# Layer 3's query norm by a block transpose and one folding product per head, and its scores scaled on ScalarE

## The chip, the cores and the metric

The kernel runs on one core of one Trainium2 chip. The metric is the time of one execution in microseconds, taken on the device; the number given is the median of several runs.

## The reference, cut to what matters

The program is four decoder layers over 1024 tokens of width 512 (8 tiles of 128 tokens). Each layer adds a gated cross attention and then a gated feed-forward to x:

```python
x = x + tanh(g_xattn[l]) * attention_l(layernorm(x), ctx)
x = x + tanh(g_ffn[l]) * ffn_l(layernorm(x))
```

The change lies in the attention of the third layer (index 2; "L2" in the code), which has 32 query heads of 128 features, 8 key heads, and per batch of 128 queries 128 keys:

```python
q = rmsnorm(hidden @ q_proj_w.T per head, q_norm_w)   # x * rsqrt(mean(x*x over 128 features) + 1e-5) * w
k = rmsnorm(ctx @ k_proj_w.T per head, k_norm_w)
scores = einsum('bhqd,bhkd->bhqk', q, k) / sqrt(128) + attention_mask
out = einsum('bhqk,bhkd->bhqd', softmax(scores), v) @ o_proj_w.T
```

The norm of a query row is one number per token and head. The kernel leaves the queries unscaled and multiplies the scores of that token by it instead; both norm weights are folded into the keys.

## The kernel before, in words

All engines run their own instruction streams, written out in Python in one order for each engine, and meet in semaphores. There is no planner: the order of the work is the order of the code. A projection splits its operands into a high and a low part (`w_hi`, `w_lo`, `xt_hi`, `xt_lo`, `a_hi`, `a_lo`) and takes three products per 128 rows of depth (`mm3`). GpSimd makes the two parts of each weight chunk (L558, L562) from a ring of 8 chunks, as soon as TensorE has freed a slot (`w_free`); SP loads the raw chunks.

An attention runs in 64 steps (`run_steps`, here with a period of 8 steps), two for each of the 32 heads: step k holds 4 of the 8 batches of head k // 2. In step k each engine does, in this order:

- TensorE (`step` in `attention`): the scores of step k into a bank of S, the turn of the probabilities of step k - 1 (`turn`, L930), the outputs of step k - 2 for two token tiles, three quarters of one half (512 tokens) of the next head's query projection into a bank of J, the outputs for the other two tiles, the last quarter of the projection, the product of the probabilities of step k - 1 with the values (`values`), and `q_squares`: for the half just projected, four products of a 128x128 block of squares (stationary) with a column of ones, which give the sum of squares per token.
- ScalarE: the copy of the turned probabilities of step k - 1 (`turned_out`), the exponentials of step k (four, each with its sum), then for the projected half the squares into `sq` (L1317) and the copy to `qT`, then `a_hi` of step k - 1 from the bank of the values.
- VectorE: four fused operations (L1816), each one batch's scores times the query norm plus the mask, the row maxima (L1824), the adds of the outputs to x for tiles 0 and 1 (L1767), the reciprocal of the sums and its product with the gate (L1846, L1849), the adds for tiles 2 and 3, and `a_lo` of step k - 1 (L1866). Between these stand, one at a time, the 12 small instructions of `query_rstd`: an integer first guess and three Newton steps (L1532 to L1540) that turn the sums of squares of one half into the norm `rq`. They are dealt out by `small(a, b)`.

The outputs of step k - 2 need `a_hi` and `a_lo` of that step: `output` waits for both. The bank of the values may be rewritten when both are made. An output for a tile waits until the tile two before it, in the same bank, has been added to x.

In the prologue of the layer (`L.first`) come values and keys, the layer norm of x, and the two halves of head 0's query.

A matmul on 4-byte data runs as two passes in the trace, so that four products with the ones are eight rows.

## Time and profile before

| | |
|---|---|
| time, three runs | 2902.35 to 2905.36 us, median 2904.11 us |
| the profiled execution: its span | 2904.7 us |
| the profiled execution: its time beside the span | not listed apart from the span |
| instructions | 47006 |
| TensorE busy | 2778.9 us, 96% |
| VectorE busy | 1728.2 us, 59% |
| ScalarE busy | 1048.6 us, 36% |
| GpSimd busy | 826.4 us, 28% |

In the profile PE is TensorE's matmul queue and PEld its weight loads, DVE is VectorE, ACT is ScalarE, POOL is GpSimd. Times are microseconds unless marked ns. Matmuls are pipelined, so that the start of one to the start of the next says what one costs. PEclk is the granted clock of TensorE as a share of full speed. A number in brackets on a timeline is the time for which the engine was idle before the instruction, with what ended the wait.

### The profile page before, as it was taken

Reading aid. Unit: us, or ns where it says so; the run is one execution under the profiler, and the core shown is the slowest. Engines: PE = TensorE matmul, PEld = TensorE weight load, DVE = VectorE, ACT = ScalarE, POOL = GpSimd, SP = SyncE. Lnnn points to the kernel's source line nnn. Section 1 sums busy time; section 2 is a strip of 40 time slices with the busy share of each in tenths; the row PEclk is TensorE's granted clock in tenths of the full one; section 3 lists DMA queues with packets and bytes.
Section 4 is the critical chain, followed back from the end, with each engine's and each line's share of the span. In section 5 each row is a group of like instructions: output and inputs, shape, how many; then the busy total and the mean of one; then the engine's idle time right before and its main releaser. Section 6 shows DMA issues by size and latency. Waiting matters only on the chain.

```text
span 2904.7 us, 47006 instructions
## 1 busy us (share of the span) xinstructions
PE 2778.9 (96%) x14928; PEld 2337.4 (80%) x14928; DVE 1728.2 (59%) x3969; ACT 1048.6 (36%) x2828; POOL 826.4 (28%) x708
## 2 busy tenths in 40 slices
PE   7997999999999998889999999999999999999998
PEld 5875888888888886667888888778878888888886
DVE  5756545544644646667777777745552555555557
ACT  3542333333333332124444444321123444444442
POOL 4011432432442431322222222245522222212200
PEclk8998999999999999999999999999999999999999
DMA  4001111111110110111111111012111000001000
GB/s 145 12 12 53 41 44 33 47 36 32 47 41 28 51 44 19 45 30 33 30 30 30 31 31 30 26 41 58 58 45 40 27 27 26 27 26 27 29 5 30
DMA packets 59826, 106.35 MB, mean 37 GB/s; under 512 B 7184, under 2 KB 11536, under 8 KB 59536
## 3 DMA queue, kind: packets, MB, share of 16 engines
q1 hardware_dynamic: 56448, 96.49, 11.6%
q10 hardware_dynamic: 3216, 7.81, 0.8%
q8 instruction: 87, 1.43, 0.2%
q14 instruction: 75, 0.61, 0.1%
HBM read 100.09 MB, written 2.10 MB: 35 GB/s over the span
## 4 chain that ended last, share of the span: by engine, by line
PE 90%; DVE 6%; ACT 2%; issue 2%; DMA 0%; POOL 0%; ACTq 0%; DVEq 0%; POOLq 0%
PE four L587 51%; PE outp L587 23%; PE value L587 9%; PE turned L930 4%; PE turned L709 1%; DVE stats L1565 1%; DVE xt_lo L1594 1%; PE turned L634 0%; DVE nt L1537 0%; DVE nt L1539 0%; DVE probs L1589 0%; DVE x L1767 0%; DVE x L1973 0%; ACT sq L1317 0%; ACT vc L1203 0%
## 5 line engine op out<-in xcount | busy, mean ns | idle before, releaser
L558 POOL TENSOR_TENSOR w_hi<-raw,zero 128x512 fp32r<-128x512 f32 x347 | 371.8, 1072 | 1926.3 <-PE four L587 896.4
L1767 DVE SCALAR_TENSOR_TENSOR x<-outp,g_inv,x 128x512 f32<-128x512 f32 x768 | 556.6, 748 | 383.5 <-PE outp L587 383.2
L562 POOL TENSOR_TENSOR w_lo<-raw,w_hi 128x512 fp32r<-128x512 f32 x352 | 454.0, 1290 | 32.3 <-ACT w_hi L1203 5.1
L587 PE MATMUL four<-xt_hi,w_lo 128*128 128x512 f32 x1024 | 424.8, 415 | 16.8 <-DVE xt_lo L1594 12.0
L587 PE MATMUL four<-xt_hi,w_hi 128*128 128x512 f32 x1024 | 406.2, 397 | 0.0
L587 PE MATMUL four<-xt_lo,w_hi 128*128 128x512 f32 x1024 | 404.4, 395 | 0.0
L587 PE MATMUL outp<-w_hi,a_lo 128*128 128x512 f32 x800 | 330.3, 413 | 14.3 <-DVE x L1767 7.5
L1203 ACT ACTIVATE pT<-turned 128x512 f32<-128x512 f32 x320 | 191.6, 599 | 345.1 <-PE turned L930 287.3
L587 PE MATMUL outp<-w_hi,a_hi 128*128 128x512 f32 x800 | 316.0, 395 | 0.0
L587 PE MATMUL outp<-w_lo,a_hi 128*128 128x512 f32 x800 | 315.3, 394 | 0.0
L1396 ACT ACTIVATE probs<-probs,top 128x128 f32<-128x128 f32 x512 | 199.6, 391 | 237.6 <-DVE top L1810 126.7
L587 PE MATMUL four<-kT,qT 128*128 (+2 forms) x1536 | 275.8, 316 | 6.5 <-issue 6.5
L1866 DVE TENSOR_TENSOR a_lo<-value,a_hi 128x512 fp32r<-128x512 f32 (+1 forms) x256 | 142.9, 558 | 190.2 <-ACT a_hi L1203 190.2
L1203 ACT ACTIVATE a_hi<-value 128x512 fp32r<-128x512 f32 (+1 forms) x256 | 126.0, 492 | 355.7 <-PE value L587 355.7
L587 PEld LDWEIGHTS four<-xt_hi,w_lo 128*128 128x128 f32 x1024 | 195.9, 191 | 56.0 <-issue 13.7
L587 PEld LDWEIGHTS four<-xt_hi,w_hi 128*128 128x128 f32 x1024 | 195.2, 191 | 44.2
L587 PEld LDWEIGHTS four<-kT,qT 128*128 128x128 f32 x1536 | 215.7, 193 | 15.3 <-issue 6.9
L587 PEld LDWEIGHTS four<-xt_lo,w_hi 128*128 128x128 f32 x1024 | 196.3, 192 | 35.0
L587 PEld LDWEIGHTS value<-pT,vc 128*128 128x128 f32 x1536 | 200.7, 191 | 22.8 <-issue 3.7
L587 PE MATMUL value<-pT,vc 128*128 128x128 f32 x1536 | 202.7, 275 | 4.8 <-ACT vc L1203 4.8
L587 PEld LDWEIGHTS outp<-w_hi,a_lo 128*128 128x128 f32 x800 | 151.0, 189 | 63.0 <-DVE x L1767 26.1
L587 PEld LDWEIGHTS outp<-w_hi,a_hi 128*128 128x128 f32 x800 | 150.8, 189 | 36.7
(259 smaller groups left out, 4627.9 us busy)
## 6 DMA issues: line engine op xcount, KB each, us to landing
raw<-in_stream SPq DMA_DIRECT2D x352, 256.0 KB, 2.6
ctx_raw<-in_ctx_t ACTq DMA_DIRECT2D x4, 512.0 KB, 6.2
x<-in_x_in ACTq DMA_DIRECT2D x2, 1024.0 KB, 11.9
kz<-kT SPq DMA_DIRECT2D x32, 64.0 KB, 2.3
pb<-in_position_bias ACTq DMA_DIRECT2D x1, 2048.0 KB, 8.7
out<-x SPq DMA_DIRECT2D x8, 256.0 KB, 2.0
qw<-in_qweight ACTq DMA_DIRECT2D x1, 768.0 KB, 3.9
ln_w<-in_ln_weight ACTq DMA_DIRECT2D x1, 256.0 KB, 2.7
```

The source lines that it names most:

```text
L558: pool.tensor_tensor(w_hi[:, k, :], raw[:, k % RAW, :], zero[:, :].to_broadcast([P, D]), ALU.add)\
L562: pool.tensor_tensor(w_lo[:, k, :], raw[:, k % RAW, :], f32(w_hi[:, k, :]), ALU.subtract)\
L587: m = pe.matmul(out_, l, r, start=start, stop=stop, skip_group_check=True)
L709: m = pe.transpose(T[:, tokens(j)], buf["pr"][:, u % 3, cols], ident[:, :])
L930: m = pe.transpose(T[:, tokens(j)], probs[:, k % 2, tokens(j)], ident[:, :])
L1203: return act.activation(dst, src, ACT.Copy)
L1396: e = act.activation(probs[:, k % 2, cols], src[:, cols], ACT.Exp, bias=top[:, k % 2, j:j + 1], scale=1.0, accum_out=sums[:, k % 2, j:j + 1])
L1565: dve.bn_stats(stats[:, b, :], x[:, b, :]).then_inc(ln_tiny, 1)
L1594: dve.tensor_tensor(xt_lo[:, :, tokens(b)], TV[b % 2][:, :].rearrange("p (k t) -> p k t", k=KT), f32(xt_hi[:, :, tokens(b)]), ALU.subtract ...
L1767: dve.scalar_tensor_tensor(out=x[:, b, :], in0=O[no_f(k) % 2][:, :], scalar=scale, in1=x[:, b, :], op0=ALU.mult, op1=ALU.add)\
L1866: dve.tensor_tensor(buf["a_lo"][:, 0:w], V[:, 0:w], f32(buf["a_hi"][:, 0:w]), ALU.subtract).then_inc(s["a_lo"], 1)
```

## The change

- **Squares in place.** ScalarE copies the projected half to `qT` first and then squares the bank of J in place, in PSUM.
- **Block transpose.** VectorE transposes that bank in 32x32 blocks into `sq` (`query_turn`) and sums each block row into 16 columns of `part`. The sums of 32 features then lie with the features' four blocks on different partitions.
- **One fold per head.** TensorE multiplies `part` (both halves, 32 columns) once per head by `fold`, a 128x128 matrix that adds the four blocks of 32 partitions. VectorE then picks each partition's own block with `own` (a multiply and a sum over four), and runs one Newton chain for the 8 columns of the head.
- **Order.** The second half of head h + 1 is projected in the even step of head h, and the first half of head h + 2 in the odd one; the first half of head 1 moves to the prologue. The fold of a head stands in an odd step, between the turn and the outputs. `query_turn` is VectorE's last work of a step, behind `a_lo`.
- **Scores.** ScalarE multiplies the four batches' scores by the norm (`scaled`, its first work of a step); VectorE adds the mask to all four in one instruction, in place of four fused operations.

```diff
         if self.name == "L2":
-            return [("q", t, 0, KT - 1), ("q", t, KT - 1, 1)]
+            return [("q", 1 - t, 0, KT - 1), ("q", 1 - t, KT - 1, 1)]
         return [("q", t // 2, t % 2 * 2, 2)]
 
+    def made_head(self, i):
+
+        return (i + 1 if self.name == "L2" else i) // self.U + 1
+
     def pieces(self, i):
 
-        return [(kind, i // self.U + 1, half) for kind, half, kt, n in self.parts(i) if kt + n == KT]
+        return [(kind, self.made_head(i), half) for kind, half, kt, n in self.parts(i) if kt + n == KT]
+
+    def sums_head(self, i):
+
+        h = (i + 1) // 2
+        return h if i % 2 and 0 < h < self.heads else 0
...
@@ -809,11 +821,14 @@
                 def bank_free(what_f, k, it):
 
                     no = L.piece[what_f(k)]
-                    if n == 2 and no > 1 and by_no[no - 1][0] == "q":
-
-                        pe.wait_ge(s["newton"], at(L, lambda i: newton_base(
-                            L, by_no[L.piece[what_f(i)] - 1]) + 1, k, it))
-                    if n == 2 and no <= B + 2 * B + 2:
+                    if n == 2 and no > 2 and by_no[no - 2][0] == "q":
+
+                        pe.wait_ge(s["q_turned"], at(L, lambda i: L.rstd[by_no[L.piece[what_f(i)] - 2]] - 2 * B,
+                                                     k, it))
+                        if by_no[no - 2][2] == 1:
+                            pe.wait_ge(s["newton"], at(L, lambda i: newton_base(
+                                by_no[L.piece[what_f(i)] - 2][1]) + 1, k, it))
+                    elif n == 2 and no <= B + 2 * B + 2:
 
                         if no > B + 4:
...
-                def q_squares(what_f, k, it):
-
-                    pe.wait_ge(s["sq"], at(L, lambda i: L.rstd[what_f(i)], k, it))
-                    bank_ = J[(L.piece[what_f(k)] + 1) % 2][:, :]
-                    for j in range(4):
-                        m = mm(bank_[:, 2 * j:2 * j + 2], buf["sq"][:, tokens(j)], ones[:, :], True, True)
-                    m.then_inc(s["qss"], 1)
+                def q_squares(head, k, it):
+
+                    pe.wait_ge(s["sq_sums"], at(L, lambda i: 2 * B + 2 * head(i) + 2, k, it))
+                    bank_ = piece_bank(L, ("q", head(k), 1))
+                    mm(bank_[:, 0:32], buf["fold"][:, :], buf["part"][:, :, :].rearrange("p t c -> p (t c)"),
+                       True, True).then_inc(s["qss"], 1)
...
-                        pe.wait_ge(s["seen"] if n in (1, 2) else s["exp"], at(L, lambda i: i - 1, k, it))
+                        pe.wait_ge(s[{1: "seen", 2: "scaled", 3: "exp"}[n]], at(L, lambda i: i - 1, k, it))
...
                     if 1 <= k <= L.NU:
                         turn(k - 1, it)
+                    if n == 2 and L.sums_head(k):
+                        q_squares(L.sums_head, k, it)
                     for no, (kind, hf, kt, kts) in enumerate(L.parts(k)):
                         if n == 2 and L.has_O(k):
                             output(k - L.lag_o, it, range(2 * no, 2 * no + 2))
                         def what_f(i, kind=kind, hf=hf):
-                            return (kind, i // L.U + 1, hf)
+                            return (kind, L.made_head(i), hf)
...
-                    if n == 2:
-                        for what in L.pieces(k):
-                            q_squares(lambda i: L.pieces(i)[0], k, it)
...
                     copy(dst, src, scale).then_inc(s["j_out"], 1)
+                    if kind == "q" and n == 2:
+                        act.activation(src, src, ACT.Square).then_inc(s["sq"], 1)
...
+                def scaled(k, it):
+
+                    act.wait_ge(s["scores"], at(L, lambda i: i + 1, k, it))
+                    act.wait_ge(s["rms"], at(L, lambda i: 2 * B + i // L.U + 1, k, it))
+                    if k >= 2:
+                        act.wait_ge(s["turned"], at(L, lambda i: i - 1, k, it))
+                    r = 2 * (k // L.U % 2) + k % 2
+                    for j in range(4):
+                        o = act.activation(probs[:, k % 2, tokens(j)], S[k % 2][:, tokens(j)], ACT.Copy,
+                                           scale=buf["rq"][:, r, j:j + 1])
+                    o.then_inc(s["scaled"], 1)
+
                 def step(k, it):
+                    if n == 2 and k < L.NU:
+                        scaled(k, it)
                     turned_out(k, it)
...
+                    dve.tensor_reduce(buf["own"][:, :], ident[:, :].rearrange("p (a i) -> p a i", a=4),
+                                      AX_X, ALU.add).then_inc(s["consts"], 1)
+                    dve.tensor_reduce(buf["fold"][:, 0:32], ident[:, :].rearrange("p (a i) -> p i a", a=4),
+                                      AX_X, ALU.add).then_inc(s["consts"], 1)
+                    dve.wait_ge(s["consts"], 3)
+                    dve.tensor_copy(buf["fold"][:, 32:64], buf["fold"][:, 0:32]).then_inc(s["consts"], 1)
+                    dve.wait_ge(s["consts"], 4)
+                    dve.tensor_copy(buf["fold"][:, 64:128], buf["fold"][:, 0:64]).then_inc(s["consts"], 1)
...
+                def query_turn(what_f, k, it):
+
+
+                    idx = at(L, lambda i: L.rstd[what_f(i)] - 2 * B, k, it)
+                    dve.wait_ge(s["sq"], at(L, lambda i: L.rstd[what_f(i)], k, it))
+                    if L.rstd[what_f(k)] > 2 * B + 1:
+                        dve.wait_ge(s["sq_sums"], at(L, lambda i: L.rstd[what_f(i)] - 1, k, it))
+                    dve.transpose(buf["sq"][:, :], piece_bank(L, what_f(k))).then_inc(s["q_turned"], 1)
+                    dve.wait_ge(s["q_turned"], idx)
+                    if what_f(k)[1]:
+                        dve.wait_ge(s["qss"], at(L, lambda i: what_f(i)[1], k, it))
+                    dve.tensor_reduce(buf["part"][:, what_f(k)[2], :],
+                                      buf["sq"][:, :].rearrange("p (c t) -> p c t", t=32), AX_X, ALU.add)\
+                        .then_inc(s["sq_sums"], 1)
+
+                STEPS = RSQRT + 2
+
+                def query_rstd(head, k, it, steps=(0, STEPS)):
+
+
+                    src = piece_bank(L, ("q", head(k), 1))[:, 0:32].rearrange("p (g c) -> p g c", c=4)
+                    rq = buf["rq"][:, 2 * (head(k) % 2):2 * (head(k) % 2) + 2, :].rearrange("p t j -> p (t j)")
+                    base = at(L, lambda i: newton_base(head(i)), k, it)
                     for j in range(*steps):
                         if j == 0:
-                            dve.wait_ge(s["qss"], at(L, lambda i: L.rstd[what_f(i)] - 2 * B, k, it))
-                            o = dve.tensor_scalar(nt[:, 0, 0:4], src, P * EPS, None, ALU.add)
+                            dve.wait_ge(s["qss"], at(L, lambda i: head(i) + 1, k, it))
+                            o = dve.scalar_tensor_tensor(
+                                out=buf["pick"][:, :, :], in0=src, scalar=P * EPS,
+                                in1=buf["own"][:, :].unsqueeze(1).to_broadcast([P, 8, 4]),
+                                op0=ALU.add, op1=ALU.mult)
                         else:
                             dve.wait_ge(s["newton"], base + j)
-                            o = rsqrt_step(j - 1, nt[:, 0, 0:4], buf["rq"][:, 2 * (h % 2) + part, :],
-                                           nt[:, 1, 0:4])
-                        o.then_inc(s["rms"] if j == RSQRT else s["newton"], 1)
+                            if j == 1:
+                                o = dve.tensor_reduce(nt[:, 0, :], buf["pick"][:, :, :], AX_X, ALU.add)
+                            else:
+                                o = rsqrt_step(j - 2, nt[:, 0, :], rq, nt[:, 1, :])
+                        o.then_inc(s["rms"] if j == STEPS - 1 else s["newton"], 1)
...
+                        if n == 2 and b == B - 1:
+                            query_turn(lambda i: ("q", 0, 0), 0, None)
                         norm_lo(norm, b)
-                    elif what[0] == "q" and n == 2:
-                        query_rstd(lambda i: what, 0, None)
+                    elif what == ("q", 0, 1) and n == 2:
+                        query_turn(lambda i: what, 0, None)
+                    elif what == ("q", 1, 0) and n == 2:
+                        query_rstd(lambda i: 0, 0, None)
+                        query_turn(lambda i: what, 0, None)
...
-                        if n == 2 and 1 <= k <= L.NU and L.pieces(k - 1):
-                            query_rstd(lambda i: L.pieces(i - 1)[0], k, it, (a, b or a + 1))
+                        if n == 2 and L.sums_head(k):
+                            query_rstd(L.sums_head, k, it, (a, b or a + 1))
...
                         elif n == 2:
 
-                            dve.wait_ge(s["rms"], at(L, lambda i: L.rstd[("q", i // L.U, i % 2)], k, it))
-                            for j in range(4):
-                                o = dve.scalar_tensor_tensor(
-                                    out=pr[:, j, :], in0=bank_[:, j, :],
-                                    scalar=buf["rq"][:, 2 * (h % 2) + k % 2, j:j + 1],
-                                    in1=buf["madd"][:, :], op0=ALU.mult, op1=ALU.add)
-                                if j == 3:
-                                    o.then_inc(s["seen"], 1)
-                                small(j)
+                            dve.wait_ge(s["scaled"], at(L, lambda i: i + 1, k, it))
+                            dve.tensor_tensor(pr, pr, buf["madd"][:, :].unsqueeze(1).to_broadcast([P, 4, P]),
+                                              ALU.add).then_inc(s["seen"], 1)
+                            small(0, 2)
                             dve.wait_ge(s["seen"], at(L, lambda i: i + 1, k, it))
                             dve.tensor_reduce(top[:, k % 2, :], pr, AX_X, ALU.max, negate=True).then_inc(s["top"], 1)
                         else:
                             dve.tensor_reduce(top[:, k % 2, 0:rows], bank_, AX_X, ALU.max, negate=True)\
                                 .then_inc(s["top"], 1)
-                        small(4)
+                        small(2)
                     if n == 2 and k < L.NU and L.has_O(k):
-                        add_tiles(k, it, range(2), lambda j: small(5 + j))
+                        add_tiles(k, it, range(2), lambda j: small(3 + j))
                     elif n == 2 and k < L.NU:
-                        small(5, 7)
+                        small(3, 5)
                     if 1 <= k <= L.NU:
                         scaled_gate(k - 1, it, small)
                     through(k, it, small)
...
                     dve.reciprocal(inv[:, u % 2, 0:rows], sums[:, u % 2, 0:rows]).then_inc(s["inv"], 1)
-                    small(7, 9)
+                    small(5, 7)
...
                     if L.has_O(k):
                         if n == 2 and k < L.NU:
-                            add_tiles(k, it, range(2, B), lambda j: small(7 + j))
+                            add_tiles(k, it, range(2, B), lambda j: small(5 + j))
                         else:
                             add_tiles(k, it)
                     elif n == 2 and k < L.NU:
-                        small(9, 11)
-                    small(11)
+                        small(7, 9)
+                    small(9, STEPS)
                     if L.has_V(k):
 
                         dve.wait_ge(s["a_hi"], at(L, lambda i: i - L.lag_v + 1, k, it))
                         w = L.nb * P
                         dve.tensor_tensor(buf["a_lo"][:, 0:w], V[:, 0:w], f32(buf["a_hi"][:, 0:w]),
                                           ALU.subtract).then_inc(s["a_lo"], 1)
+                    if n == 2 and L.pieces(k):
+                        query_turn(lambda i: L.pieces(i)[0], k, it)
                     tail_stats(k)
 
                 if n == 1:
                     dve.wait_ge(pb_in, 16)
-                    dve.wait_ge(s["m_ready"], 1)
```

## Rows read from the trace of the kernel before

**Rows 1.** The page, part 1: busy us, share of the span, instructions of each engine.
```profile
PE 2778.9 (96%) x14928; PEld 2337.4 (80%) x14928; DVE 1728.2 (59%) x3969; ACT 1048.6 (36%) x2828; POOL 826.4 (28%) x708
```

**Rows 2.** The page, part 4: the chain that ended last, by engine.
```profile
PE 90%; DVE 6%; ACT 2%; issue 2%; DMA 0%; POOL 0%; ACTq 0%; DVEq 0%; POOLq 0%
```

**Rows 3.** Stretches: length, busy us of PE, PEld, DVE, ACT, POOL, PEclk, DMA.
```profile
1340.38:1863.11 522.73, 517.74 (x3019) 441.76 (x3018) 408.53 (x1392) 228.56 (x704) 133.50 (x117) 1.00 0.10 30
1863.11:1894.00 30.89, 24.02 (x126) 18.67 (x125) 23.73 (x54) 7.63 (x26) 5.12 (x5) 1.00 0.11 26
```

**Rows 4.** Timeline of TensorE: start, us, line, operation, operands, count, idle before.
```profile
1510.10 1.05 PE L587 MATMUL value<-pT,vc 128*128 128x128 f32 x8
1511.02 1.05 PE L587 MATMUL four<-ones,sq 128*128 128x2 f32 x8
1511.94 1.14 PE L587 MATMUL four<-kT,qT 128*128 x8
1512.91 0.60 PE L930 MATMUL turned<-ident,probs 128*128 128x128 f32 x4
1513.27 0.48 PE L587 MATMUL outp<-w_hi,a_lo 128*128 128x512 f32 x1
...
1518.92 1.06 PE L587 MATMUL value<-pT,vc 128*128 128x128 f32 x8
...
1887.85 0.47 PE L587 MATMUL outp<-w_hi,a_lo 128*128 128x512 f32 x1 [1.61 <-DVE a_lo L1866]
```

**Rows 5.** Groups in 1340.3 to 1863.2: shapes, count, busy us, mean ns, idle before.
```profile
L1396 ACT ACTIVATE probs<-probs,top 128x128 f32<-128x128 f32 x232 | 90.5, 391 | 97.2 <-DVE top L1824 97.2
L1816 DVE SCALAR_TENSOR_TENSOR probs<-four,rq,madd 128x128 f32<-128x128 f32 x232 | 77.7, 345 | 43.0 <-PE four L587 27.6 <-issue 15.4
...
L1824 DVE TENSOR_REDUCE top<-probs 128x4 f32<-128x512 f32 x58 | 39.8, 686 | 0.0
```

**Rows 6.** Waits in 1340.3 to 1863.2: waiter, releaser, us, times, longest.
```profile
PEld outp L587 <- DVE x L1767: 14.8, 54, 0.5
```

**Rows 7.** Timeline of ScalarE in the step of rows 4.
```profile
1511.34 0.60 ACT L1203 ACTIVATE a_hi<-value 128x512 fp32r<-128x512 f32 x1
```

**Rows 8.** Timeline of VectorE: key stage, the step of rows 4, the stage's end.
```profile
1230.86 1.14 DVE L1537 TENSOR_TENSOR nt<-rk 128x8 f32<-128x8 f32 x1
...
1511.98 0.69 DVE L1866 TENSOR_TENSOR a_lo<-value,a_hi 128x512 fp32r<-128x512 f32 x1 [1.18 <-ACT a_hi L1203]
...
1514.58 0.69 DVE L1824 TENSOR_REDUCE top<-probs 128x4 f32<-128x512 f32 x1
1515.18 0.15 DVE L1539 SCALAR_TENSOR_TENSOR nt<-nt 128x4 f32<-128x4 f32 x1
...
1519.13 0.71 DVE L1539 SCALAR_TENSOR_TENSOR nt<-nt 128x4 f32<-128x4 f32 x1
1519.88 0.16 DVE L1540 SCALAR_TENSOR_TENSOR rq<-nt,rq 128x4 f32<-128x4 f32 x1
1520.80 0.69 DVE L1866 TENSOR_TENSOR a_lo<-value,a_hi 128x512 fp32r<-128x512 f32 x1 [0.76 <-ACT a_hi L1203]
...
1886.91 0.69 DVE L1866 TENSOR_TENSOR a_lo<-value,a_hi 128x512 fp32r<-128x512 f32 x1 [0.77 <-ACT a_hi L1203]
```

**Rows 9.** Timeline of GpSimd in the key stage and the step of rows 4.
```profile
1230.67 1.30 POOL L562 TENSOR_TENSOR w_lo<-raw,w_hi 128x512 fp32r<-128x512 f32 x1
...
1518.78 1.04 POOL L558 TENSOR_TENSOR w_hi<-raw,zero 128x512 fp32r<-128x512 f32 x1 [13.03 <-PE four L587]
1519.90 1.27 POOL L562 TENSOR_TENSOR w_lo<-raw,w_hi 128x512 fp32r<-128x512 f32 x1
```

**Rows 10.** Groups by line and shape, whole span: VectorE's 512-wide kinds not above.
```profile
L1805 DVE TENSOR_TENSOR probs<-probs,m 128x512 f32<-128x512 f32 x64 | 67.4, 1054 | 2.2
...
L1589 DVE TENSOR_SCALAR probs<-x,mv,rstd 128x512 f32<-128x512 f32 x64 | 35.0, 556 | 0.3
...
L1684 DVE TENSOR_REDUCE nt<-sq 128x4 f32<-128x512 f32 x16 | 10.9, 678 | 6.7 <-ACT sq L1317 6.7
```

More of the change, by code:

```diff
@@ L386, in build @@
             A2["qk_w"] = sb("qk_w", [P, 2], F32, st)
+            A2["fold"] = sb("fold", [P, P], F32, st)
+            A2["own"] = sb("own", [P, 4], F32, st)
+            A2["part"] = sb("part", [P, 2, 16], F32, st)
+            A2["pick"] = sb("pick", [P, 8, 4], F32, st)
         with ExitStack() as st:
@@ L463, in build @@
                         "a_hi a_lo outp x_acc"),
-            sems("_L1", common + " seen masked clamp sum m_ready r2 added"),
-            sems("_L2", common + " seen vc qss sq ksum newton rms k_turned k_out wqk"),
+            sems("_L1", common + " seen masked clamp sum ready added"),
+            sems("_L2", common + " seen vc qss sq sq_sums newton rms k_turned k_out consts "
+                        "q_turned scaled"),
             sems("_L3", common + " vc"),
```

63 lines of the change are left out of this document (28 added, 35 removed).

## The prediction

> **What bounds the kernel now.** I read the page first. TensorE is busy for 2778.9 us of the 2904.7 us span, VectorE for 1728.2 [rows 1], and the chain that ended last lies on TensorE for 90% [rows 2]. An average over eight stages cannot price a change in one of them, so I next took the windows of the changed stage, layer 3's attention: from 1340.38 us to 1863.11 us TensorE is busy for 517.74 of 522.73 us, VectorE for 408.53, ScalarE for 228.56, at a granted clock of 1.00 [rows 3]. That window holds 58 steps, counted by its 58 row maxima [rows 5], so a step takes 522.73 / 58 = 9.01 us.
>
> Then I read one step on TensorE's timeline, from the start of one product with the values to the next, 1510.10 to 1518.92 [rows 4]. I call the start v. Values take 0.92, the four products with the ones (eight passes) 0.92, scores 0.97, the turn of the probabilities 0.36, and outputs with projections 5.65 (1513.27 to 1518.92). That is 8.82 us with TensorE never waiting for long; the other 0.19 us of the mean are small waits, mostly for VectorE's adds (14.8 us over the window) [rows 6]. So TensorE's own work sets the step now. The reader is to see one more thing: the products with the ones stand behind the values and ahead of the next outputs. While they run, ScalarE makes a_hi and VectorE a_lo, which the outputs need. They are work, and also cover.
>
> **What leaves TensorE.** 0.92 us in each step, 1.84 us in a pair of steps; one folding product per pair comes back. It is two passes, at 0.92 / 8 each: 0.23 us.
>
> **Wait one, each even step: a_lo.** Without the squares TensorE stands at the outputs at v + 0.92 + 0.97 + 0.36 = v + 2.25. ScalarE still does two evacuations of the query bank (now qT, then the square) ahead of a_hi, so a_hi starts at 1511.34 [rows 7], v + 1.24, and a_lo at 1511.98, v + 1.88 [rows 8]. How long the outputs then take to start is seen at the end of the stage, where TensorE does wait for it: a_lo starts at 1886.91 and the output at 1887.85, 0.94 us later [rows 4, 8]. So the output starts at v + 2.82: a wait of 0.57 us that the squares hid. The even step is at least 2.82 + 5.65 = 8.47 us.
>
> **Wait two, each odd step: the fold.** The second half of a head's query is projected in an even step, and its sums are folded in the next odd step, on TensorE between the turn and the outputs. VectorE does the block transpose and the sum over blocks after a_lo, in program order, and the fold waits for both; queued behind the fold are that step's outputs and projections. a_lo starts at v + 1.88; an independent VectorE instruction follows 0.60 after a 512-wide one (1514.58 to 1515.18 [rows 8]), so the transpose starts at v + 2.48. The trace has no block transpose. The nearest rows read 512 columns: 0.56 us for a scaled subtraction from SBUF, 0.68 for the key sums [rows 10], 0.69 for a_lo from PSUM [rows 8]. I take 0.69, since it too reads PSUM; ends 0.40 (below every row) and 1.25 (nearly double). Then 0.04 to a dependent instruction (1519.84 to 1519.88 [rows 8]) and 0.68 for the sum: v + 3.89. From VectorE's end to TensorE's first pass 0.25 (1887.60 to 1887.85): the fold starts at v + 4.14, against v + 2.25 for TensorE's arrival, a wait of 1.89 us. With its 0.23 and 5.65 the odd step is 10.02 us.
>
> The Trainium skill (VectorE: DVE Perf Modes, "The three transpose paths") gives a VectorE transpose of 128x128 bf16 as 311 ns; no run here shows that. If all of it grew with the columns, 512 of them would be an estimated 1.24 us, and by this the odd step would be 0.55 us longer.
>
> **Wait three: the end of the Newton chain.** It runs once per pair, in the odd step, and is two instructions longer (a selecting multiply and a sum over blocks). Where two followed the last add to x, five do now, one right behind it and four more, all ahead of the next a_lo. What that costs is shown by the step ending at w = 1518.92. GpSimd splits a chunk there: w_hi from 1518.78 for 1.04, w_lo from 1519.90 for 1.27 [rows 9]. The first small instruction behind the add (1519.13) takes 0.71 and ends at 1519.84, with w_hi; the next slips into the gap (1519.88, 0.16) [rows 8]. A third would be issued at about 1520.08, inside w_lo. In the key stage such a one, issued at 1230.86, took 1.14 and ended with GpSimd's 1230.67 plus 1.30 [rows 8, 9]. So the third ends near 1521.20 and the last near 1521.60; a_lo starts at about 1521.54 (w + 2.62) instead of 1520.80 (w + 1.88). That is 0.74 more for the following even step: 9.21 us. A chunk of q is now freed at the end of even steps and one of the output weights at the end of odd ones, so GpSimd works in both; in the even case a_lo, transpose and block sum stand there, and a_lo ran 0.69 under w_lo at 1520.80 [rows 8], unhindered. Ends for this term: 0 (GpSimd later or earlier) and 0.95 (one more instruction held for its split).
>
> **What else moves, at no cost, and its cover.** ScalarE's four scalings wait for the scores, which end at v + 2.06, and for the norm; behind them on ScalarE stand the copy of pT and the exponentials. At the 0.39 us of an exponential of the same shape [rows 5] they end by v + 3.62, and VectorE reaches the mask add at v + 3.89 anyway. In even steps the norm ends with the chain, near w + 2.7: the scalings end at w + 4.26, VectorE's block sum at w + 4.63. If this cover goes, the exponentials come later; with 0.69 for the add and for the maximum they end at v + 3.89 + 0.69 + 0.69 + 1.56 = v + 6.83, and the next turn needs them beyond v + 9. The mask add has two SBUF inputs; layer 2's similar add has a mean of 1.05 [rows 10], and four fused operations cost 4 x 0.345 [rows 5]: between 0.33 less and 0.69 less, and in the same slack. VectorE's busy time, 408.53 / 58 = 7.04 us a step, loses 1.38 and half a chain and gains about 0.69 three times: under 8.47, so it becomes no bound. The square written in place in PSUM has no row; I take the 0.60 of a_hi's copy [rows 7].
>
> The Trainium skill (ScalarE: Activation LUTs, "Step-by-step: what each stage is for") says that ScalarE writes PSUM faster than SBUF; no run here shows it. By it a_hi could start sooner, but not before the values end (v + 1.05 against v + 1.24), so both waits would shrink by at most 0.19: 11 us in all.
>
> The piece that moves ahead of the loop is missing at its end, and the added constants are made under earlier products: 0, with 4 us either way.
>
> **The sum.** A pair takes 9.21 + 10.02 = 19.23 us against 2 x 9.01 = 18.03: 1.20 us more, times 29 pairs = 35 us. The execution profiled has a span of 2904.7, 0.6 above the median of the runs shown (2904.1), so they are one level: 2904 + 35 = **2939 us**.
>
> **Rivals.** *A, the chain's end is not held by GpSimd:* the even step is 8.47, the pair 18.49, +0.46 x 29 = 13 us: 2917. For it: GpSimd's start depends on when a chunk is freed. Against: its place behind the last projection is unchanged.
> *B, TensorE's saving shows (faster):* VectorE has the sums ready before the turn, and only a_lo is waited for. Pair 2 x 8.47 = 16.94, -1.09 x 29 = -32: 2872. For it: TensorE is 96% busy and loses work. Against: the order of VectorE's queue, a_lo first; it decides from a fold ready by v + 2.6, when a_lo itself has only just ended.
> *C, no change:* A with a short transpose. The pair is 18.03 if transpose and sum together take 0.46 less than taken, a transpose of 0.23; with the chain's end at 0 and a transpose of 0.4 it is 18.20, +5 us: 2909.
> *D, a slow transpose (1.25):* +0.56 in odd steps and about 0.3 in even ones, where tile 2 then waits for the add of tile 0: +25 us more, 2964.
> A fall of the clock is no rival: from 1863.11 to 1894.00 TensorE is busy for 24.02 of 30.89 us and keeps 1.00 [rows 3].
>
> **Chances.** Forecast 0.45, A 0.22, D 0.12, C 0.10, B 0.11. The range 2908 to 2960 holds the forecast, A and part of C and D. A measurement of this kernel tells about 0.2% (6 us) from no change: faster 0.12, same 0.10, slower 0.78.
>
> **What would show it.** TensorE idle before the folding product, released by VectorE's block sum, near 1.9 us in 31 steps; TensorE idle before the first output, released by a_lo, in even steps; a small VectorE instruction of over 1 us at the end of odd steps; transposes near 0.69. It is wrong if the fold finds its sums ready, or if VectorE's block operations take under half a microsecond together.

## The result and the profile after

The changed kernel takes 2933.12 us (median of four runs, 2929.41 to 2935.63) against 2903.28 us for the kernel before in the same session: a ratio of 1.0101, 95% interval 1.0087 to 1.0116. The change made the kernel 29 us slower; 2939 had been predicted. The profiled execution has a span of 2933.8 us (its time: 2935.63), 29.1 above the span before.

The page of the changed kernel, parts 1 and 4, answers to [rows 1, 2]:

```profile
PE 2730.7 (93%) x14480; PEld 2287.2 (78%) x14480; DVE 1775.0 (61%) x3557; ACT 1114.9 (38%) x3084; POOL 826.3 (28%) x707
...
PE 82%; DVE 10%; ACT 3%; issue 3%; DMA 0%; ACTq 0%; POOL 0%; DVEq 0%; POOLq 0%
```

TensorE lost 48 us of work and the kernel became longer: part of the last chain went from TensorE (90 to 82%) to VectorE (6 to 10%). In the changed stage TensorE, which had waited for little but the adds [rows 6], now waits in every step. The waits between 1330 and 1890 us (waiter, releaser, us in total, times, longest):

```profile
PEld four L599 <- DVE part L1749: 52.1, 29, 1.9
DVE a_lo L1924 <- ACT a_hi L1217: 46.9, 30, 1.6
...
PE four L599 <- DVE part L1749: 45.2, 29, 1.6
PEld outp L599 <- issue: 37.3, 29, 1.3
PE outp L599 <- DVE a_lo L1924: 30.7, 29, 1.1
```

The folding product (`four`, released by the block sum `part`) waits 45.2 / 29 = 1.56 us in each odd step, the first output 30.7 / 29 = 1.06 us in each even one. An odd step and the start of the even one behind it, on TensorE (answers to [rows 4]):

```profile
1506.68 1.05 PE L599 MATMUL value<-pT,vc 128*128 128x128 f32 x8
1507.57 1.06 PE L599 MATMUL four<-kT,qT 128*128 x8
1508.46 0.60 PE L945 MATMUL turned<-ident,probs 128*128 128x128 f32 x4
1510.60 0.41 PE L599 MATMUL four<-part,fold 128*128 128x32 f32 x2 [1.54 <-DVE part L1749]
1510.84 0.48 PE L599 MATMUL outp<-w_hi,a_lo 128*128 128x512 f32 x1
...
1516.48 1.05 PE L599 MATMUL value<-pT,vc 128*128 128x128 f32 x8
1517.37 1.06 PE L599 MATMUL four<-kT,qT 128*128 x8
...
1519.94 0.49 PE L599 MATMUL outp<-w_hi,a_lo 128*128 128x512 f32 x1 [1.08 <-DVE a_lo L1924]
```

and on VectorE (answers to [rows 8]):

```profile
1508.51 0.69 DVE L1924 TENSOR_TENSOR a_lo<-value,a_hi 128x512 fp32r<-128x512 f32 x1 [1.56 <-ACT a_hi L1217]
1509.12 0.70 DVE L1745 STREAM_TRANSPOSE sq<-four 128x512 f32<-128x512 f32 x1
1509.86 0.69 DVE L1749 TENSOR_REDUCE part<-sq 128x16 f32<-128x512 f32 x1
1510.46 0.68 DVE L1878 TENSOR_TENSOR probs<-probs,madd 128x512 f32<-128x512 f32 x1
...
1516.70 0.63 DVE L1565 SCALAR_TENSOR_TENSOR nt<-nt 128x8 f32<-128x8 f32 x1
1517.37 0.17 DVE L1566 SCALAR_TENSOR_TENSOR rq<-nt,rq 128x8 f32<-128x8 f32 x1
1517.57 1.14 DVE L1563 TENSOR_TENSOR nt<-rq 128x8 f32<-128x8 f32 x1
1518.74 0.17 DVE L1565 SCALAR_TENSOR_TENSOR nt<-nt 128x8 f32<-128x8 f32 x1
1518.94 0.17 DVE L1566 SCALAR_TENSOR_TENSOR rq<-nt,rq 128x8 f32<-128x8 f32 x1
1519.03 0.68 DVE L1924 TENSOR_TENSOR a_lo<-value,a_hi 128x512 fp32r<-128x512 f32 x1
```

beside GpSimd's split at the end of that odd step (answers to [rows 9]):

```profile
1516.27 1.04 POOL L570 TENSOR_TENSOR w_hi<-raw,zero 128x512 fp32r<-128x512 f32 x1 [6.57 <-PE four L599]
1517.39 1.29 POOL L574 TENSOR_TENSOR w_lo<-raw,w_hi 128x512 fp32r<-128x512 f32 x1
```

Read the three together. In the odd step a_lo, transpose and block sum stand one behind the other on VectorE, and the fold starts 0.05 us behind the last. At the step's end the third small instruction takes 1.14 us where its like takes 0.16 to 0.17, and ends with GpSimd's split (1517.39 + 1.29); the next a_lo and the next output are late by it. It is the same in every odd step of the stage: 58 of these small instructions, two in each, take 0.63 to 1.14 us, and each of them ends 0.02 to 0.03 us behind the end of one of GpSimd's operations.

From the scores of one step to those of the next, the odd step takes 9.80 us (1507.57 to 1517.37) and the even one 9.13: a pair of 18.93. Read in the same way, the ordinary steps before take 8.82 and 8.96 us, a pair of 17.78. But one step in eight took 10.08 to 10.41 us before, about 1.24 more than its like. There VectorE's loop of eight steps jumps back (the loop's turn, below), and the profile shows VectorE idle with no releaser, in six such rows; the first is shown here, with TensorE's wait behind it. After, there is no such row, and the turn costs nothing. Twice, though, TensorE's clock falls in the stage after, for 1.68 us each time; the second fence has one of the two stretches (its ends and length, busy us of PE, PEld, DVE, ACT and POOL, granted clock).

Of the kernel before, VectorE at the loop's turn, and TensorE behind it:

```profile
1397.18 0.35 DVE L1816 SCALAR_TENSOR_TENSOR probs<-four,rq,madd 128x128 f32<-128x128 f32 x1 [2.76 <-issue]
1397.65 0.50 PE L587 MATMUL four<-xt_hi,w_lo 128*128 128x512 f32 x1 [1.00 <-DVE nt L1712]
```

Of the kernel after, one of the two stretches at a lower clock:

```profile
1416.03:1419.02 2.99, 2.99 (x9) 2.31 (x8) 1.97 (x8) 1.52 (x8) 0.00 (x0) 0.50 0.00 0
```

So the 29.1 us are: 28 pairs from step 4 to step 60 by 1.15, +32; six turns of the loop, -7.4; the clock, +3.4; which makes 28, and the scores' times bear it out (1340.38 and 1345.51 us at step 4; 32.9 us apart at step 60). The stage starts 5.1 us later and its tail is 3.8 us shorter. In the prologue, where no other work covers it, the new Newton chain stands beside GpSimd's splits, and five of its instructions take 0.98 to 1.14 us, as the one below. That this is the late start's cause was not tried, and another cause stands beside it: from 1290 us to step 4 the mean granted clock is 0.82, against 0.93 before. It is 0.50 from 1296.3 to 1303.1 and from 1313.3 to 1327.0, with TensorE busy for 5.78 and 7.66 us; before, it is 0.50 from 1311.0 to 1317.8, with 5.41 us busy. With 0.43 us a product instead of 0.23 (as in the stage, last section), the 8.0 us more come to an estimated 3.7 us. Some of both offsets differs between executions of the same code: the kernel of experiment 11, which is the changed kernel outside VectorE's loop, reaches step 4 at 1343.43 us, and its tail is 4.5 us longer than the changed kernel's.

```profile
1307.26 1.14 DVE L1563 TENSOR_TENSOR nt<-rq 128x8 f32<-128x8 f32 x1
```

### The profile page after: what moved, and what is told of

It reads as the page before. It is cut to its first block, busy times and chain, and to the rows that moved or that the text cites. A ratio compares the mean times of both kernels' runs of the same rounds, so it can differ in the third digit from the quotient of the medians.

```text
span 2933.8 us, 45790 instructions
## 1 busy us (share of the span) xinstructions
PE 2730.7 (93%) x14480; PEld 2287.2 (78%) x14480; DVE 1775.0 (61%) x3557; ACT 1114.9 (38%) x3084; POOL 826.3 (28%) x707
## 4 chain that ended last, share of the span: by engine, by line
PE 82%; DVE 10%; ACT 3%; issue 3%; DMA 0%; ACTq 0%; POOL 0%; DVEq 0%; POOLq 0%
PE four L599 47%; PE outp L599 23%; PE value L599 7%; PE turned L945 3%; DVE nt L1563 2%; PE turned L721 1%; DVE nt L1565 1%; DVE a_lo L1924 1%; DVE sq L1745 1%; DVE part L1749 1%; ACT a_hi L1217 1%; DVE stats L1591 1%; ACT qT L1217 1%; DVE x L1829 1%; DVE xt_lo L1620 1%
## 5 line engine op out<-in xcount | busy, mean ns | idle before, releaser
L574 POOL TENSOR_TENSOR w_lo<-raw,w_hi 128x512 fp32r<-128x512 f32 x352 | 454.2, 1290 | 31.9 <-ACT w_hi L1217 4.6
L599 PE MATMUL four<-kT,qT 128*128 (+2 forms) x1536 | 268.1, 311 | 5.9 <-issue 5.9
L599 PEld LDWEIGHTS four<-xt_hi,w_lo 128*128 128x128 f32 x1024 | 197.3, 193 | 52.2 <-issue 15.4
L599 PE MATMUL four<-w_hi,ct_lo 128*128 128x512 f32 x416 | 170.2, 409 | 11.9 <-POOL w_lo L574 6.7
```

Source lines behind the costliest of these rows:

```text
L574: pool.tensor_tensor(w_lo[:, k, :], raw[:, k % RAW, :], f32(w_hi[:, k, :]), ALU.subtract)\
L599: m = pe.matmul(out_, l, r, start=start, stop=stop, skip_group_check=True)
```

## The experiments

Medians, and ratios to the kernel before with their 95% intervals:

| | us | ratio |
|---|---|---|
| changed kernel | 2933.12 | 1.0101 (1.0087 to 1.0116) |
| 1 fold later | 2895.47 | 0.9970 (0.9959 to 0.9982) |
| 2 chain early | 2914.44 | 1.0035 (1.0024 to 1.0047) |
| 3 both | 2884.19 | 0.9932 (0.9915 to 0.9948) |
| 4 projection first, chain early | 2864.67 | 0.9866 (0.9849 to 0.9882) |
| 5 fused operations back | 2956.08 | 1.0187 (1.0167 to 1.0207) |
| 6 short transpose | 2913.66 | 1.0039 (1.0028 to 1.0050) |
| 7 transpose first | 2912.84 | 1.0032 (1.0020 to 1.0044) |
| 8 before, projection first | 2939.98 | 1.0126 (1.0106 to 1.0145) |
| 9 projection first alone | 2873.14 | 0.9891 (0.9875 to 0.9908) |
| 10 as 4, fused operations back | 2903.73 | 0.9998 (0.9989 to 1.0008) |
| 11 long loop body | 2952.83 | 1.0158 (1.0135 to 1.0180) |
| 12 as 8, sums read first | 2921.54 | 1.0056 (1.0040 to 1.0073) |

The runs come from four sessions, in which the kernel before took 2902.82 to 2905.09 us, so differences between two rows are good to some 2 us.

**1: the fold behind the first two outputs.** One place later on TensorE, all else as it was.

```diff
-                    if n == 2 and L.sums_head(k):
+                    if n == 2 and L.sums_head(k) and not L.parts(k):
                         q_squares(L.sums_head, k, it)
...
                             output(k - L.lag_o, it, range(2 * no, 2 * no + 2))
+                        if n == 2 and no == 0 and L.sums_head(k):
+                            q_squares(L.sums_head, k, it)
```

> The changed kernel with the folding product moved on TensorE from ahead of the first two outputs to behind them; nothing else. Theory (TensorE waits in each odd step for the block transpose and sum): the fold then finds its sums ready, only the wait for a_lo is left (output at v + 2.74), the odd step falls from 9.80 to 2.74 + 5.64 + 0.24 = 8.62 us, 1.18 x 30 = 35 us less: about 2898 us. Rival (VectorE's load has become the bound of the step): its work is the same, so the time stays near 2933. Rival (the norm's Newton chain, which now starts later, becomes late for the next scaling): part of the gain is lost, about 2910.

Measured 2895.47, 38 us below the changed kernel. The odd step is 8.64 us instead of 9.80, and no wait for the block sum is left; of TensorE's waits this one remains:

```profile
PE outp L599 <- DVE a_lo L1926: 38.8, 55, 1.1
```

The fold's wait was the largest term, and it was the place of the fold that made it: two outputs later its sums are ready. The odd step's 1.16 us by 29 are 34 of the 38 us; the two falls of the clock, absent here, are 3.4 more.

**2: the end of the Newton chain early.** Four of the five small instructions at the end of the odd step move behind the product with the gate, where VectorE waits for TensorE's next output.

```diff
                         .then_inc(s["g_inv"], 1)
+                    small(7, 11)
...
-                            add_tiles(k, it, range(2, B), lambda j: small(5 + j))
+                            add_tiles(k, it, range(2, B), lambda j: small(9 + j))
...
-                        small(7, 9)
-                    small(9, STEPS)
+                        small(11, STEPS)
```

> The changed kernel with four of the Newton chain's instructions moved from the end of the odd step to behind the gate's product, where VectorE waits for an output; nothing else. Theory (the last ones stand under GpSimd's split and make a_lo late): a_lo starts at w + 1.83 instead of w + 2.55, the output of the even step follows at w + 2.74 instead of w + 3.46, 0.72 x 30 = 22 us less: about 2911 us. Rival (only the fold costs time, the late a_lo is hidden by something else): 2933. Rival (VectorE is the bound): 2933.

Measured 2914.44, 19 us below. The even step falls from 9.13 to 8.40 us, and its wait for a_lo from 27.4 us (26 times, 1345 to 1840 us) to:

```profile
PE outp L599 <- DVE a_lo L1924: 9.6, 27, 0.4
```

**3: both.**

> Both edits of the two kernels before in one. Theory: the two waits are in different steps and add up: 2933 - 35 - 22 = 2876 us, which is also below the kernel before (2903), since TensorE's 1.8 us of squares per pair are gone and what is left of the waits is 0.6 us per step for a_lo. Rival (the chain, started later by the moved fold and dealt out earlier, meets itself and waits): about 2890.

Measured 2884.19: 49 us of the 56 that the two gave apart, and between theory and rival. Every step now takes 8.6 to 8.7 us and still waits for a_lo:

```profile
PE outp L599 <- DVE a_lo L1926: 28.5, 56, 0.7
```

**6: a short transpose.** The transpose moves 32 of the 512 columns; the kernel leaves out the rest of it, all else runs.

```diff
-                    dve.transpose(buf["sq"][:, :], piece_bank(L, what_f(k))).then_inc(s["q_turned"], 1)
+                    dve.transpose(buf["sq"][:, 0:32], piece_bank(L, what_f(k))[:, 0:32]).then_inc(s["q_turned"], 1)
```

> The changed kernel with a block transpose of 32 of the 512 columns (the query norms are then wrong: most of the transpose is left out); everything else stands. Theory (transpose and sum stand between a_lo and the fold, and TensorE waits for them): a transpose of some 0.2 instead of 0.71 us makes the fold 0.5 us earlier in each odd step and leaves even steps as they are: 0.5 x 30 = 15 us less, about 2918. Rival (the fold waits for something else, as the norm's chain or the bank): 2933. Rival (VectorE's total sets the step): 0.5 x 60 = 30 less, 2903.

Measured 2913.66. The transpose in this kernel and in the changed one (ns, least, median, most):

```profile
L1745 DVE STREAM_TRANSPOSE sq<-four x64: 201/206/216, 1294.1 to 1866.4; 128x32 f32<-128x32 f32 x64
```

```profile
L1745 DVE STREAM_TRANSPOSE sq<-four x64: 702/706/717, 1295.0 to 1888.9; 128x512 f32<-128x512 f32 x64
```

0.50 us less of transpose, and the odd step falls by 0.50, from 9.80 to 9.30: it lies whole on the path to the fold. By 29 that is 15 of the 19 us; the falls of the clock, absent here, are 3.4 more.

**7: in even steps the transpose ahead of a_lo.**

```diff
                     small(9, STEPS)
+                    if n == 2 and k % 2 == 0 and L.pieces(k):
+                        query_turn(lambda i: L.pieces(i)[0], k, it)
...
-                    if n == 2 and L.pieces(k):
+                    if n == 2 and k % 2 and L.pieces(k):
```

> The changed kernel with the transpose and sum ahead of a_lo on VectorE in even steps (those whose half is folded next), behind it in odd ones as now. Theory (it is the place in VectorE's queue that makes the sums late): the squares are ready at v + 1.28, the sums at v + 2.75, so the fold starts at v + 2.8; a_lo is now the later one, at v + 2.67, and the outputs start at v + 3.58; the odd step is 9.22 instead of 9.80, 0.58 x 30 = 17 us less: about 2916. Rival (one wait only takes the place of the other, with nothing gained): 2933.

Measured 2912.84. The fold's wait shrinks to 12.6 / 27 = 0.47 us, and a_lo is late in the odd step as well: one wait is paid in part with another, since both products stand behind one queue.

```profile
PE outp L599 <- DVE a_lo L1926: 38.7, 54, 1.1
PE four L599 <- DVE part L1749: 12.6, 27, 0.6
```

**4 and 9: the projection ahead of the outputs.** TensorE does three quarters of the projection, the fold and outputs 0 and 1, then the last quarter and outputs 2 and 3; in 4 with the chain early, in 9 without.

```diff
...
                     for no, (kind, hf, kt, kts) in enumerate(L.parts(k)):
-                        if n == 2 and L.has_O(k):
-                            output(k - L.lag_o, it, range(2 * no, 2 * no + 2))
...
-                        if n == 1 and L.has_O(k):
+                        if n == 2 and no == 0 and L.sums_head(k):
+                            q_squares(L.sums_head, k, it)
+                        if n in (1, 2) and L.has_O(k):
                             output(k - L.lag_o, it, range(2 * no, 2 * no + 2))
```

> The changed kernel with the chain dealt out early, and on TensorE the three quarters of the projection ahead of the first two outputs, the fold between them, the last quarter ahead of the other two outputs. Theory (all three waits are for VectorE results that come 1 to 2 us too late): 2.07 us of projection cover both a_lo and the fold; a step is TensorE's own 7.8 us, the pair 15.8 against 19.03, 3.2 x 29 = 93 us less: about 2840 us. Rival (VectorE, with some 7.5 us of work in an odd step, then sets it): odd steps of 8.3 to 8.5, about 2855.

> The changed kernel with the projection ahead of the outputs and the chain where the change left it. Theory: the projection covers the waits for a_lo and for the fold alike, so that moving the chain adds little, and VectorE sets the pace: 2865 to 2872. Rival: the chain's end, held beside GpSimd, still sets when the outputs start: 2884 (19 us above the version with both edits).

Measured 2864.67 and 2873.14: 4 is the fastest version of all, 1.3% below the kernel before. It missed the 2840 of its theory, and the 2855 of the rival too. Busy us of PE, PEld, DVE, ACT and POOL in 480 us of the stage, of 4 and then of the changed kernel:

```profile
1350.00:1830.00 480.00, 465.41 (x2602) 389.66 (x2602) 454.80 (x1016) 287.46 (x936) 132.92 (x115) 1.00 0.11 32
```

```profile
1350.00:1830.00 480.00, 414.65 (x2269) 348.90 (x2269) 390.42 (x882) 251.29 (x815) 115.97 (x100) 0.99 0.09 27
```

VectorE is busy for 95% of the stretch in 4 (373.75 of 480 us before the change), and in 9 for 456.87 us. But it is not the bound throughout, as the rival had it: TensorE is busy for 97%. In an ordinary odd step of 4, 8.00 us, TensorE never waits; in an even one, 8.38 us, it is busy for 8.05 and waits 0.33 for VectorE's adds (0.74 in 9). The theory had taken TensorE's own work for 7.8 us a step. The projection covers the waits for a_lo and for the fold alike.

**5: the scores' half undone.** The four fused operations come back on VectorE, ScalarE's scalings go.

```diff
...
-                    if n == 2 and k < L.NU:
-                        scaled(k, it)
...
-                            dve.wait_ge(s["scaled"], at(L, lambda i: i + 1, k, it))
-                            dve.tensor_tensor(pr, pr, buf["madd"][:, :].unsqueeze(1).to_broadcast([P, 4, P]),
-                                              ALU.add).then_inc(s["seen"], 1)
+                            dve.wait_ge(s["rms"], at(L, lambda i: 2 * B + i // L.U + 1, k, it))
+                            for j in range(4):
+                                o = dve.scalar_tensor_tensor(
+                                    out=pr[:, j, :], in0=bank_[:, j, :],
+                                    scalar=buf["rq"][:, 2 * (h % 2) + k % 2, j:j + 1],
+                                    in1=buf["madd"][:, :], op0=ALU.mult, op1=ALU.add)
+                            o.then_inc(s["seen"], 1)
```

> The changed kernel with the scores' half undone: VectorE's four fused operations as before, no scaling on ScalarE; the query norm by transpose and fold stays. Theory (all that the change costs comes from the query norm's half): VectorE's maximum is some 0.45 us later per step, within the slack ahead of the adds, so the time stays near 2933, within 5 us. Rival (the scaling on ScalarE lengthens the way to the exponentials and costs part of the 30 us): 2915. Rival (VectorE is the bound after the change, so that the one mask add is worth its 0.45 us in each step): 2960.

Measured 2956.08, 23 us above the changed kernel: a miss of the theory, and the rival's time came for another reason than the rival's. The ordinary steps are 9.23 and 9.80 us, 0.10 more in a pair, 3 us in all. The rest stands at six places, where a step takes 11.81 to 14.43 us; VectorE and TensorE at the first:

```profile
1406.63 1.13 DVE L1876 SCALAR_TENSOR_TENSOR probs<-four,rq,madd 128x128 f32<-128x128 f32 x4 [2.48 <-issue]
```

```profile
1409.19 0.50 PE L599 MATMUL outp<-w_hi,a_lo 128*128 128x512 f32 x1 [2.54 <-DVE x L1827]
```

It is the turn of VectorE's loop again, and TensorE waits longer behind it than it did before the change. Together these six steps are 21.7 us longer than their like: 2.6 to 2.8 us each for the first three, 4.1 to 5.2 for the others, where TensorE's clock falls behind the wait (a mean of 0.60 to 0.79 in the 8 us around it). From one branch to the next the trace has 364 VectorE instructions before the change, 287 after and 322 here, waits and register instructions counted. That gave the next theory.

**11: the changed kernel with a long loop body.** Only waits that are long fulfilled are added, twelve in each step; in the trace they are 48 instructions more in eight steps, 335 in all.

```diff
+                    if n == 2 and it is not None:
+                        for _ in range(12):
+                            dve.wait_ge(s["seen"], 1)
                     if L.has_O(k):
```

> The changed kernel, with waits on a semaphore that is long past its value added to VectorE's loop of layer 3, ahead of the adds for tiles 2 and 3: VectorE's loop body grows from 287 instructions to 335 (322 with the four fused operations back, 364 before the change); no other work. Theory (the loop's turn): VectorE stands still at the turn of a long loop body and not at that of the changed kernel's short one. Expected: a gap of about 2.5 us with no releaser at the first VectorE instruction behind each of six turns, TensorE waiting about 3 us behind each, +20 us: 2953 (2946 to 2958). Rival: the gap belongs to the four fused operations or to what they wait for. Then there is no gap here, and the added waits stand where VectorE waits for TensorE's next output anyway: 2933 to 2938.

Measured 2952.83, the time of the theory. The gap stands at all six turns and nowhere else (2.29 to 2.47 us). The six steps are 17.4 us longer than their like, 2.1 to 2.2 each where the clock holds and 3.6 to 3.8 in the three where it falls behind the wait, so TensorE's wait itself is shorter than the 3 us expected:

```profile
1406.32 0.69 DVE L1878 TENSOR_TENSOR probs<-probs,madd 128x512 f32<-128x512 f32 x1 [2.47 <-issue]
```

```profile
1408.44 0.55 PE L599 MATMUL outp<-w_hi,a_lo 128*128 128x512 f32 x1 [2.12 <-DVE x L1829]
```

So the gap belongs to the length of the loop's body and not to the fused operations. The Trainium skill (Runtime: NRT & Kernel Launch, "Instruction fetch mechanics") has a rule of this kind: an engine's instructions stream through a small buffer in blocks of 256, and a taken branch to a place outside the two blocks at hand waits for a fetch. The gaps agree with it in kind; where between 287 and 322 instructions they begin, and whether the body's place in those blocks matters, no run shows.

**10: 4 with the fused operations back.**

> The version with the projection first and the chain early (2864.67 us), with the four fused operations back in place of ScalarE's scalings and the mask add. Theory (VectorE sets the pace there, 95% busy, and the turn of the long body costs again): (1.12 - 0.68) x 62 = +27 us of VectorE's work and about 2.5 us at each of seven turns, +17: 2909 (2895 to 2915). Rival: the scalings are worth the loop's turn alone: 2882. Rival: they are worth nothing: 2865.

Measured 2903.73, no different from the kernel before. A pair is 16.83 us against 16.38 (+13 us in 29), and the gap of 2.55 to 2.78 us is back at six turns, whose steps are 25 us longer than their like in all. In the best version the scores' half of the change is worth 39 us.

**8 and 12: the kernel before with the projection first.** Would the reordering alone do as much? In 8 the outputs move behind the projection and the weight chunks change order with them; 12 moves, besides, the read of the sums ahead of the fused operations.

```diff
-            if name != "L2":
+            if True:
                 for what in self.pieces(i):
...
-                        if n == 2 and L.has_O(k):
-                            output(k - L.lag_o, it, range(2 * no, 2 * no + 2))
...
-                        if n == 1 and L.has_O(k):
+                        if n in (1, 2) and L.has_O(k):
```

> The kernel before with TensorE's order of the best kernel so far (three quarters of the projection ahead of the first two outputs); the order of two weight chunks in the stream follows. Theory (before, the squares already hid a_lo, so there is no wait for the projection to cover): the time stays near 2904, within 6 us; what the reordered kernel gained then belongs to the change together with the order. Rival (the order is worth the same by itself): the small waits for VectorE's adds go and it falls by 10 to 15 us, or more.

Measured 2939.98, 37 us slower than the kernel before: a miss of both theories. In that kernel the sums of squares lie in the bank that the projection wants next, and VectorE reads them (`nt`) only behind its first fused operation. Outputs ahead of the projection had covered that, but for 1.00 us at a turn. An ordinary step of 8, and one at a loop's turn:

```profile
1388.55 0.50 PE L587 MATMUL four<-xt_hi,w_lo 128*128 128x512 f32 x1 [0.17 <-DVE nt L1710]
1400.61 0.58 PE L587 MATMUL four<-xt_hi,w_lo 128*128 128x512 f32 x1 [3.12 <-DVE nt L1710]
```

The second edit, in 12:

```diff
+                            small(0)
                             dve.wait_ge(s["rms"], at(L, lambda i: L.rstd[("q", i // L.U, i % 2)], k, it))
...
-                                small(j)
+                                if j:
+                                    small(j)
```

> The kernel before with the projection ahead of the outputs (2939.98 us), and the first small instruction of the norm, which reads the sums of squares out of the projection's bank, moved ahead of the four fused operations. Theory: there the projection waits for that read, which stood behind the first fused operation, 0.17 and 0.48 us by turns and about 3 us at a loop's turn. Without the ordinary waits the pair falls from 18.53 towards 17.78, -0.75 x 29 = -22 us; the wait at the loop's turn stays: 2918 (2905 to 2925). Rival: the projection waits for something else (the order of VectorE's adds): 2935 to 2945.

Measured 2921.54: the pair falls from 18.53 to 18.03, 15 of the 22 us expected, and a turn still costs 2.5 to 5.6 us. So in the forms tried the reordering pays only with the change. The reason is read from the waits and was not tried by itself: with the change the block transpose frees the bank by the end of the step, and the short loop body takes the gap away.

## Why the prediction was right, step by step

- *What leaves TensorE*: as said; the fold costs 1510.84 - 1510.60 = 0.24 (0.23). But values and scores follow at 0.89 each, not at the 0.92 and 0.97 of [rows 4], so TensorE stands ready at v + 2.14 and not at v + 2.25.
- *Wait one*: with the chain out of the way (2) the even step is 8.40 us, where 8.47 was the floor.
- *Wait two*: mis-sized by 0.22. The fold starts at v + 3.92, not v + 4.14, and the odd step is 9.80, not 10.02. The transpose takes 0.706 (0.69 taken), the sum 0.686. What was off is the hand-over, from VectorE's end to TensorE's start: 0.25 was read from a_lo to an output, and holds there (1519.71 to 1519.94 is 0.23); from the block sum to the fold it is 0.05. Experiments 1 and 6 show the wait and its parts.
- *Wait three*: as said; the third instruction is held for 1.14 us to the end of GpSimd's w_lo, a_lo starts at w + 2.55 (2.62), the even step is 9.13 (9.21). Experiment 2 shows that the chain's end costs it; that GpSimd's operations hold the instructions is read from the 58 ends that fall together.
- *What else moves, at no cost*: this step failed. Cover and durations held (the mask add takes 0.68, the four scalings 1.14), but the scores' half was not free of effect: it shortened VectorE's loop. That took away the 7.4 us that the turns had cost before; with the query norm's half alone they cost 21.7 (5), and with a longer body put back 17.4 (11).
- *The sum*: 1.20 us by 29 pairs against 1.15. The two sides were not alike: 9.01 was a mean over the stage, with six turns of 1.24 us in it, the 19.23 had no turn. Like for like it would have been 19.23 - 17.78 = 1.45 by 29, +42, and 2946. Setting the one against the other took the turns to be gone, which they were, for a reason that the prediction didn't know: in that the 2939 was lucky. Of the 0.19 us a step that it put to VectorE's adds, 0.13 were the turns (7.4 / 58), and their gaps stand in [rows 5] ("issue 15.4"). The waits were taken 0.30 a pair too long, 8 us in all; the falls of the clock (+3.4) and the late start less the shorter tail (+1.3) gave part of it back.
- *Prologue and tail*: +5.1 and -3.8, where 0 with 4 either way was given; 1.3 together. Neither was explained by the prediction.
- *Rivals*: A and B fall by the two waits, C with A, D by the 0.706. The fall of the clock, dismissed there, came twice in the stage. The stretch it was dismissed by ends at 1894.00; from 1894.60 to 1898.00 the kernel before shows 0.51.

The Trainium skill (VectorE: DVE Perf Modes, "The three transpose paths") would by the estimate have given 1.24 us for 512 columns; the trace says 0.706, and 0.206 for 32, so a fixed part doesn't grow with the columns and the measurement decides. By the Trainium skill (ScalarE: Activation LUTs, "Step-by-step: what each stage is for") the square written to PSUM should have been quicker than one written to SBUF; it takes 0.59 against 0.60 for the copy to SBUF beside it, and 0.59 for the next one, so the trace shows no such gain:

```profile
1516.68 0.60 ACT L1217 ACTIVATE qT<-four 128x512 f32<-128x512 f32 x1 [2.94 <-PE four L599]
1517.18 0.59 ACT L1357 ACTIVATE four<-four 128x512 f32<-128x512 f32 x1
1517.69 0.59 ACT L1217 ACTIVATE a_hi<-value 128x512 fp32r<-128x512 f32 x1
```

## What to carry to other kernels

Work taken from the busiest engine is also cover for what stands behind it: before it goes, place the product that depends on another engine late enough, as 1 and 4 did: in 4 the same change gains 1.3% instead of losing 1%. Compare steps of like kind, and look for the one step in a loop that differs: what an edit does to the length of a loop's body can be worth as much as what it does to the work. When a reordering pays in one version, ask which bank or buffer it needs free before taking it to another (8).

## What the runs showed of the hardware

- VectorE stands still for 2.3 to 2.8 us at the turn of a loop of 322, 335 or 364 instructions, and not for one of 287 (nor, in layer 2, for one of 183). How much of it a step feels depends on what TensorE has queued: where the clock holds, 1.24 us a turn before the change, 2.1 to 2.2 in 11, 2.5 to 2.8 in 5 and 12; where it falls behind the wait, up to 5.6 (12).
- A block transpose of 128x512 4-byte values from PSUM takes 0.706 us, of 128x32 0.206.
- VectorE's small instructions between SBUF tiles (0.17 us) take up to 1.14 us beside GpSimd's split and end with it, 58 times in the stage, while a_lo, which also reads PSUM, and the transpose run at their usual 0.69 and 0.70 inside one, 28 times each.
- TensorE's granted clock was 0.50, the lower of its two levels (1.2 of 2.4 GHz), from 1416.03 to 1419.02 us and again from 1644.60 to 1647.59; a product took 0.43 us there instead of 0.23. In the 4.75 us ahead of the first fall TensorE had been busy for 3.12, with a wait of 1.63 for the fold besides. Steps with the same wait elsewhere in the stage kept 1.00.
